# Wide cross attention with 77 keys a head laid out in 80 rows instead of 96, on one NeuronCore of Trainium2

## The reference

```python
def _L1_xattn_ref(x, context, ln_gamma, ln_beta, w_q, w_kv, w_out, b_out, gate):
    NUM_HEADS, DIM_HEAD = 16, 64
    xn = _layernorm(x, ln_gamma, ln_beta)
    q = (xn @ w_q).reshape(B, SQ, NUM_HEADS, DIM_HEAD)
    k, v = jnp.split(context @ w_kv, 2, axis=-1)
    ...
    scores = jnp.einsum('bqhd,bkhd->bhqk', q * DIM_HEAD ** (-0.5), k)
    attn = jax.nn.softmax(scores, axis=-1)
    out = jnp.einsum('bhqk,bkhd->bqhd', attn, v).reshape(B, SQ, INNER)
    out = out @ w_out + b_out
    return out * jnp.tanh(gate[0])
...
x = x + _L1_xattn_ref(_layernorm(x, axis=-1), ctx_1024, ...)
```

## Time and profile before

| what | value |
|---|---|
| median of 3 runs | 1561.71 us (1556.27 to 1563.02) |
| span of the profiled execution | 1523.6 us |
| median less that span | 38.1 us |
| busy: TensorE / ScalarE / VectorE / GpSimd | 93% / 55% / 60% / 43% |
| the stage's steps, from the first values to the last weighted sum | from 1008 to 1371 us of the span |
| share of the chain that ended last, L3137 / L3103 / L3128 | 6% / 6% / 3% |

### The profile page before, as it was taken

The page is one execution under the profiler, slowest core; times in us unless marked ns, Lnnn a source line. Parts: engine busy times, 40 slices in busy tenths (PEclk is TensorE's granted clock), DMA queues, the critical chain, the costliest instruction groups (busy, mean ns, idle before and its releaser), DMA issues.

```text
span 1523.6 us, 38875 instructions
## 1 busy us (share of the span) xinstructions
PE 1419.2 (93%) x14805; PEld 1097.5 (72%) x14805; DVE 920.5 (60%) x2386; ACT 837.5 (55%) x1622; POOL 660.8 (43%) x678
## 2 busy tenths in 40 slices
PE   6999999996999999999699998899999999998997
PEld 5776767675777876887466666678888888885864
DVE  3334444434789975434679998775666767656223
ACT  4545554443777875545267776555555556542531
POOL 3244444334234652006677876532234444433034
PEclk9999999998999999999789999999999999999999
DMA  5020320000357632237000000000000000001323
GB/s 160 17 64 8 100 92 28 8 5 1 142 203 274 229 130 72 78 118 274 19 12 2 2 2 2 14 2 6 7 6 8 11 11 7 9 11 41 103 69 87
DMA packets 97824, 92.65 MB, mean 61 GB/s; under 512 B 21869, under 2 KB 71658, under 8 KB 97386
## 3 DMA queue, kind: packets, MB, share of 16 engines
q1 hardware_dynamic: 93034, 80.71, 16.3%
q0 software_dynamic: 4608, 9.45, 2.0%
HBM read 31.92 MB, written 58.21 MB: 59 GB/s over the span
## 4 chain that ended last, share of the span: by engine, by line
PE 57%; issue 14%; POOL 13%; DVE 8%; ACT 4%; DMA 2%; SPq 1%; POOLq 0%; DVEq 0%; ACTq 0%
PE bank L3137 6%; PE bank L3103 6%; PE bank L3097 4%; PE bank L3116 4%; PE bank L1538 4%; POOL s_p L1217 4%; PE bank L1554 4%; PE bank L3128 3%; PE bank L854 2%; PE bank L2505 2%; PE bank L2515 2%; PE bank L874 2%; POOL s_level L467 2%; PE bank L827 2%; POOL s_rows L3564 2%
## 5 line engine op out<-in xcount | busy, mean ns | idle before, releaser
L2887 POOL TENSOR_TENSOR s_p<-s_p,s_inverse 128x616 f32<-128x616 f32 x64 | 78.3, 1229 | 221.5 <-DVE s_inverse L3024 221.5
L1324 ACT COPY s_pT<-bank 77x512 f32<-77x512 f32 (+1 forms) x256 | 135.1, 584 | 71.0 <-PE bank L1538 70.7
L1538 PE MATMUL bank<-ident,s_p 128*77 128x128 f32 (+1 forms) x1024 | 142.2, 287 | 17.0 <-ACT s_p L1315 10.3
L1538 PEld LDWEIGHTS bank<-ident,s_p 128*77 128x77 f32 (+1 forms) x1024 | 117.8, 149 | 45.7 <-ACT s_p L1315 28.9
L1217 POOL TENSOR_TENSOR s_p<-s_p,s_peak 128x1024 f32<-128x1024 f32 x64 | 120.2, 1898 | 33.9 <-DVE s_peak L1408 33.9
L1315 ACT ACTIVATE s_p<-s_p 128x616 f32<-128x616 f32 (+1 forms) x128 | 111.2, 889 | 32.2 <-POOL s_p L1217 27.7
L720 DVE TENSOR_TENSOR s_aT<-bank,s_weight 128x512 f32<-128x512 f32 x64 | 44.3, 692 | 98.8 <-PE bank L864 82.3
L3008 DVE TENSOR_REDUCE s_peak<-bank 128x8 f32<-128x616 f32 x64 | 50.7, 792 | 79.3 <-PE bank L3116 79.3
L2944 ACT ACTIVATE s_p<-s_p 128x616 f32<-128x616 f32 x64 | 46.5, 727 | 82.0 <-DVE s_p L3012 81.9
L1394 DVE TENSOR_TENSOR s_p<-bank,pos_bias 128x1024 f32<-128x1024 f32 x64 | 77.6, 1217 | 21.4 <-PE bank L1527 21.4
L3103 PE MATMUL bank<-pos_bias,s_ctx 128*32 128x128 f32 x3072 | 90.5, 274 | 0.0
(11 more groups left out here) (363 smaller groups left out, 3543.3 us busy)
## 6 DMA issues: line engine op xcount, KB each, us to landing
sorted_tokens<-s_zero SPq DMA_DIRECT2D x4, 5632.0 KB, 19.6
sorted_tokens<-s_zero SPq DMA_DIRECT2D x8, 2560.0 KB, 16.3
routed_tokens<-s_routed SPq DMA_DIRECT2D x24, 256.0 KB, 2.4
s_tokens<-sorted_tokens SPq DMA_DIRECT2D x48, 64.0 KB, 1.8
s_rows<-sorted_tokens SPq DMA_DIRECT2D x48, 64.0 KB, 1.8
x_all<-x SPq DMA_DIRECT2D x8, 256.0 KB, 3.1
w_s_gateup<-s_gateup SPq DMA_DIRECT2D x1, 2048.0 KB
out<-x_all SPq DMA_DIRECT2D x8, 256.0 KB, 2.6
```

What stands on the lines that cost most here:

```text
L1324: nc.scalar.copy(pT[0:keys, b % 2, 4 * q:4 * q + 4, :].rearrange("m h t -> m (h t)"), bank[0:keys, flip_bank("p", b, q), :]).then_inc(drai ...
L1538: last = nc.tensor.transpose(bank[0:keys, into, j * T:(j + 1) * T], p[:, b % 2, 4 * q + j, :], core.ident[:, :])
L2887: nc.gpsimd.tensor_tensor(part, part, inverse[:, b % 2, heads].unsqueeze(2).to_broadcast([P, HU, M]), ALU.mult).then_inc(share_ready, 1)
```

## The change

A head takes `MP` = 80 rows instead of 96, so the 16 heads take 10 tiles instead of 12, in three banks of 4, 4 and 2 tiles (`BANKS5`). 80 rows are two and a half pieces of 32: 8 of the 40 lane pieces of a batch lie across two heads. Such a piece is made by two products that accumulate into the same lane, each with zero columns where the other has keys; for that the context has 16 zero columns ahead of its 77 (`LEFT`) and 19 behind. `lane_pieces()` deals the products of each lane out in turns.

```diff
-MP = 96
+MP = 80
 QUAD = 4
 TILES5 = H * MP // P
-PER_QUAD = TILES5 // QUAD
+LEFT = 16
+WIDE = LEFT + 3 * LANE
+BANKS5 = [range(k, min(k + QUAD, TILES5)) for k in range(0, TILES5, QUAD)]
+LAST5 = len(BANKS5) - 1
...
 def lane_pieces():
-    per_head = MP // LANE
-    return [(k // 4, LANE * (k % 4), k // per_head, LANE * (k % per_head)) for k in range(QUAD * per_head)]
+    lanes = [[] for _ in range(LANES)]
+    for k in range(TILES5 * LANES):
+        head, row = divmod(LANE * k, MP)
+        if row + LANE <= MP:
+            lanes[k % LANES].append((k // LANES, head, LEFT + row, True, True))
+        else:
+            lanes[k % LANES].append((k // LANES, head, LEFT + row, True, False))
+            lanes[k % LANES].append((k // LANES, head + 1, LEFT + row - MP, False, True))
+    return [(LANE * lane, *piece) for turn in zip(*lanes, strict=True) for lane, piece in enumerate(turn)]
...
             for step in range(BATCH + 2):
-                for q in range(QUAD):
+                for q in range(len(BANKS5)):
                     if q % 2 == 0 and step < BATCH:
                         exp_of(step, q // 2)
                     if 1 <= step <= BATCH:
                         keep_values(step - 1, q)
                 for q in range(QUAD):
-                    if 1 <= step <= BATCH:
+                    if 1 <= step <= BATCH and q < len(BANKS5):
                         keep_pT(step - 1, q)
                     if heads_in(step):
                         keep_key(step // G + 1, heads_in(step)[q])
...
-            def values_of(b, q):
-                into, g = ring.fill(pe, "v", b, q), b // G
-                for tile, lane, head, row in lane_pieces():
-                    last = nc.tensor.matmul(bank[lane:lane + LANE, into, tile * D:(tile + 1) * D],
-                                            ctx[:, g % 3, b % G, row:row + LANE], vo[:, QUAD * q + head, :],
-                                            start=True, stop=True, tile_position=(0, lane))
-                last.then_inc(filled, 1)
+            def values_of(b):
+                g, into = b // G, {}
+                for k, (lane, tile, head, column, start, stop) in enumerate(pieces):
+                    q = tile // QUAD
+                    if q not in into:
+                        into[q] = ring.fill(pe, "v", b, q)
+                    last = nc.tensor.matmul(bank[lane:lane + LANE, into[q], tile % QUAD * D:(tile % QUAD + 1) * D],
+                                            ctx[:, g % 3, b % G, column:column + LANE], vo[:, head, :],
+                                            start=start, stop=stop, tile_position=(0, lane))
+                    if k == ends[q]:
+                        last.then_inc(filled, 1)
...
             def flip_p(b, q):
-                pe.wait_ge(share_ready, 2 * b + q // 2 + 1)
+                pe.wait_ge(share_ready, 2 * b + (1 if q == 0 else 2))
...
-                for j in range(PER_QUAD):
+                for j in BANKS5[q]:
...
             def weigh(b):
-                pe.wait_ge(drained, max(place["p", b, QUAD - 1], place["v", b, QUAD - 1]) + 1)
+                pe.wait_ge(drained, max(place["p", b, LAST5], place["v", b, LAST5]) + 1)
```

More of the change, by code:

```diff
@@ L2781, in stage5, with values @@
         folded_away = (w.s5_wvT, w.s5_wo, w.s1_wq, w.s1_wk)
-        def values(b, q):
-            return folded_away[b % 2 * 2 + q // 2][:, q % 2 * PER_QUAD:(q % 2 + 1) * PER_QUAD, :]
+        def values(b, tiles):
+            first = tiles[0] % H1
+            return folded_away[b % 2 * 2 + tiles[0] // H1][:, first:first + len(tiles), :]
         sem = core.plain_semaphore
@@ L2828, in stage5 @@
             for q in range(QUAD):
-                if step:
+                if step and q < len(BANKS5):
                     take("p", step - 1, q)
@@ L2853, in _ @@
                 if g >= 3:
[L2854 to L2855 removed]
+                    sp.wait_ge(filled, place["v", G * (g - 2) - 1, LAST5] + 1)
+                sp.dma_start(ctx[:, g % 3, :, LEFT:LEFT + M],
                              ctxT_dram[:, g * GM:(g + 1) * GM].rearrange("c (n m) -> c n m", m=M)
@@ L2930, in keep_values @@
                     act.wait_ge(weighed, b - 1)
-                nc.scalar.copy(values(b, q).rearrange("p j d -> p (j d)"),
-                               bank[:, ring_bank("v", b, q), 0:PER_QUAD * D]).then_inc(drained, 1)
+                nc.scalar.copy(values(b, BANKS5[q]).rearrange("p j d -> p (j d)"),
+                               bank[:, ring_bank("v", b, q), 0:len(BANKS5[q]) * D]).then_inc(drained, 1)
             def keep_pT(b, q):
@@ L2937, in keep_pT @@
                     act.wait_ge(weighed, b - 1)
-                nc.scalar.copy(pT[:, b % 2, PER_QUAD * q:PER_QUAD * (q + 1), :].rearrange("p j t -> p (j t)"),
-                               bank[:, ring_bank("p", b, q), 0:PER_QUAD * T]).then_inc(drained, 1)
+                tiles = BANKS5[q]
+                nc.scalar.copy(pT[:, b % 2, tiles[0]:tiles[0] + len(tiles), :].rearrange("p j t -> p (j t)"),
+                               bank[:, ring_bank("p", b, q), 0:len(tiles) * T]).then_inc(drained, 1)
             def exp_of(b, u):
@@ L3010, in soften @@
                 if b >= 2:
-                    dve.wait_ge(filled, place["p", b - 2, QUAD - 1] + 1)
+                    dve.wait_ge(filled, place["p", b - 2, LAST5] + 1)
                 nc.vector.tensor_tensor(p[:, b % 2, heads, 0:M].rearrange("p (g j) m -> p g j m", j=QUAD), scores,
@@ L3097, in key_of @@
                 nc.tensor.matmul(bank[:, into, 0:GM].rearrange("p (n m) -> p n m", m=M), kq[:, h, :],
-                                 ctx[:, g % 3, :, 0:M], start=True, stop=True).then_inc(filled, 1)
-            def values_of(b, q):
-                into, g = ring.fill(pe, "v", b, q), b // G
-                for tile, lane, head, row in lane_pieces():
-                    last = nc.tensor.matmul(bank[lane:lane + LANE, into, tile * D:(tile + 1) * D],
-                                            ctx[:, g % 3, b % G, row:row + LANE], vo[:, QUAD * q + head, :],
-                                            start=True, stop=True, tile_position=(0, lane))
-                last.then_inc(filled, 1)
+                                 ctx[:, g % 3, :, LEFT:LEFT + M], start=True, stop=True).then_inc(filled, 1)
+            pieces = lane_pieces()
+            ends = [max(k for k, piece in enumerate(pieces) if piece[1] in tiles) for tiles in BANKS5]
+            def values_of(b):
[9 more added lines that the diff above has]
+                        last.then_inc(filled, 1)
             def scores_of(b):
@@ L3123, in flip_p @@
             def flip_p(b, q):
-                pe.wait_ge(share_ready, 2 * b + q // 2 + 1)
+                pe.wait_ge(share_ready, 2 * b + (1 if q == 0 else 2))
                 into = ring.fill(pe, "p", b, q)
-                flat = p[:, b % 2, QUAD * q:QUAD * (q + 1), :].rearrange("p h m -> p (h m)")
-                for j in range(PER_QUAD):
-                    last = nc.tensor.transpose(bank[:, into, j * T:(j + 1) * T], flat[:, j * P:(j + 1) * P],
-                                               core.ident[:, :])
+                flat = p[:, b % 2, :, :].rearrange("p h m -> p (h m)")
+                for j in BANKS5[q]:
+                    last = nc.tensor.transpose(bank[:, into, j % QUAD * T:(j % QUAD + 1) * T],
+                                               flat[:, j * P:(j + 1) * P], core.ident[:, :])
                 last.then_inc(filled, 1)
             def weigh(b):
-                pe.wait_ge(drained, max(place["p", b, QUAD - 1], place["v", b, QUAD - 1]) + 1)
+                pe.wait_ge(drained, max(place["p", b, LAST5], place["v", b, LAST5]) + 1)
                 if b:
@@ L3137, in weigh @@
                     last = nc.tensor.matmul(bank[:, OUT, 0:D], pT[:, b % 2, j, :],
-                                            values(b, j // PER_QUAD)[:, j % PER_QUAD, :], start=(j == 0),
+                                            values(b, [j])[:, 0, :], start=(j == 0),
                                             stop=(j == TILES5 - 1))
@@ L3156, in _ @@
                 if 1 <= step <= BATCH:
-                    for q in range(QUAD):
-                        values_of(step - 1, q)
+                    values_of(step - 1)
                 for q in range(QUAD):
-                    if 1 <= step <= BATCH:
+                    if 1 <= step <= BATCH and q < len(BANKS5):
                         flip_p(step - 1, q)
```

5 lines of the change are left out of this document (3 added, 2 removed).

## The result

The changed kernel takes 1552.80 us (median of 13 runs, 1544.53 to 1556.74) against 1562.02 us of the kernel before (13 runs): a ratio of 0.9945, with a 95% interval of 0.9932 to 0.9959. The forecast of 1552.8 us was met, and the gain is just above the half per cent that I had named as what can be told from no change.

What follows compares the result with a forecast made beforehand. TensorE was taken as the bound, with ScalarE's ring of banks able to hold it up. Weighted sum -14.3, transposes and keys +5.9, step 1 -0.3, steps without keys -0.2: -8.9 us, so 1552.8 us, range 1546 to 1560.

Steps and rivals of the forecast that it cites:

- The weighted sum: 10 products for 12 on TensorE, four instructions fewer a batch, counting in full: -14.3 us in 32 batches.
- The values: Same 48 products and 96 instructions a batch on TensorE, 2.76 us as before: no change.
- the slower rival: Accumulating products of pieces across two heads wait for each other: 1566 to 1616 us; chance 5%.
- ScalarE's queue: Times after first values instruction: values copies start 1.37, 2.47 and 3.56, second exponential 2.94, last copy done 3.93 us.
- The rival with a larger fixed cost: ScalarE copies: all 0.265 us of the shortest fixed, each copy 0.1 us longer, 8.1 us lost: 1561 us; chance 3%.
- Transposes and keys: TensorE's turns in the 27 steps with keys: 0.11 us gained, 0.33 lost to stalls, 0.22 longer each: +5.9 us.
- p1's stall: Second transpose group waits for the last values copy, behind the second exponential on ScalarE: 0.19 us a step.
- The second stall: Third key waits for ScalarE's copy of the second transpose group: 0.14 us a step.
- Two transposes less are worth 0.11: In a step with keys, two transposes fewer on TensorE save 0.11 us, against 0.33 of stalls.
- Steps without keys: Steps 28 to 32: transposes end almost as before (-0.03 us a step), last weighted sum about 0.1 earlier; together -0.2 us.
- The 38.1 us around the span: Time outside the profiled 1523.6 us span, against the 1561.71 us median; taken to stay unchanged.
- No stalls: Rival: ScalarE early enough that TensorE never waits in the ring, 8.9 us come back: 1543.9 us; chance 13%.

Runs made afterwards that it cites:

- the run with both waits removed: The change with both exponentials ahead of the values copies on ScalarE and ring turns p0 k0 p1 k1 k2 p2 k3: 1539.93 us, ratio 0.9869 to the kernel before.

## Why the prediction was right, point by point

The mechanism was right: the removed products of the weighted sum count in full, and the ring takes part back at the two places named, p1 behind v2 and e1, and k2 behind the copy of p1. That the median came out at 1552.8 us to the hundredth is luck: two terms of the sum were off by 0.14 us a step or more each and cancelled, and the profiles show less of a gain than the times do.

- **The weighted sum** is worth what was said: 2.23 us in the chain, and 13.3 us alone (forecast 14.3).
- **The values** stay at 2.76 us. Products that accumulate into the same lane four products apart do not wait for each other; the slower rival is out.
- **ScalarE's queue** was right to 0.01 us at all five points. The copy of 256 columns, which no row of before showed, takes 0.363 us for the values (0.372 forecast by the straight line), as the groups of copies by shape show; that of transposes takes 0.382:

```profile
L2951 ACT COPY s_pT<-bank 128x512 f32<-128x512 f32 x64 | 37.4, 595 | 0.3 <-PE bank L3148 0.2
...
L2943 ACT COPY w_s_k<-bank 128x256 f32<-128x256 f32 x16 | 5.8, 363 | 0.0
```

 The rival with a larger fixed cost is out. The Trainium skill's page "ScalarE: Activation LUTs" (Rules for kernel authors) budgets about 0.3 us plus 0.83 ns an element for an ACTIVATE whose bias is a pointer operand; worked out for 256 columns that would be, as an estimate, 0.51 us. The instruction here is a COPY and takes 0.363.
- **Transposes and keys**: the forecast net of +0.22 us a step was measured as +0.24 (0.45 less in the weighted sum, 0.21 less in all), but two of its numbers were off and cancelled. A group of four transposes takes 0.44 us and not 0.49: the 0.123 came from a run of twelve. So without stalls the step would have been shorter, 10.42 and not 10.56. And p1's stall is 0.33 and not 0.19: k0 ends at 3.77, not 3.87, and p1's loads come 0.12 us after the copy's end, where I had taken 0.03 from a key. The second stall, 0.14, was 0.13 to 0.16. Together the stalls cost 0.49 and not 0.33.
- **"Two transposes less are worth 0.11"** was too little. From 11.12 to 10.42 us the step loses 0.70, of which 0.45 is the weighted sum; the 0.25 left are the two transposes and the 0.06 that e1 had cost before. The 0.11 came from pricing the transposes of after at 0.123 and taking those of before as measured, about 0.11 each; the forecast's "19 to 20 us" for all removed products price the two at about 0.2. The 0.14 that is missing here (3.8 us in 27 steps) stands against the 0.16 that is missing in the stalls. In the kernel before, where the ring was in balance, the run with one transpose in p3 shows them to be worth nothing.
- **Steps without keys** were sized wrong: steps 28 and 29 gain 0.26 us each instead of 0.48 (9.89 and 10.03 before, 9.63 and 9.77 after). Step 30, without routing at its end, gains 0.45 as forecast. In the other two the routing's products at the step's end use the ring as well, and wait for the copies of p behind e1, which I had followed only to the last transpose:

```profile
1368.80 0.97 PEld L3442 LDWEIGHTS bank<-w_s_routerT,w_s_w2T 128*128 128x128 f32 x8 [0.22 <-ACT s_pT L2951]
```

- **The 38.1 us around the span** were an artefact of holding one execution against a median of others. The sum stood on the steps and took no harm.
- **No stalls** (13%) did not come about by itself; the run with both waits removed shows what it would have been, 1539.9 us and not 1543.9; its steps without keys and its hole are shorter too. The Trainium skill's page "Perfetto Trace Analysis" (Optimization Strategy) says that consistent bubbles can mean too little SBUF or PSUM for the next tile. The trace agrees in so far as the gaps stand at the same two places in every step with keys, with a ring of three banks. But both went by another order, without a further bank, and no run here tries a further one.

The sum of -8.9 us stands against 9.2 us measured (6.4 to 10.6 by the interval), of which the stage's profiles show 6.6: the steps with keys gave 5.5 instead of 6.0, and the end of the stage 1.1 instead of 2.9, where the hole took 1.2 us more than in the second profile of before and steps 28 and 29 fell short by 0.4. No row shows the rest of 2.6 us. To the end of the program the profiles show only 3.9 to 5.4 us, less than the interval's lower end; what is missing lies ahead of the fifth stage or between executions, and its cause stays open.

## What to carry to other kernels

Where an engine fills a small ring of banks and another empties it, time taken off the filling engine counts in full outside the turns of the ring. Inside, it can be lost to a wait, as in p3 of before; see how long a bank is away (fill, hand over, copy, hand back) and put at least that much other work between two uses. Wider copies empty more at a time, but the first comes later, so what stands between them in the emptying engine's queue can move onto the path: here an exponential that cost 0.06 us a step before cost 0.33 after. Two reorderings without a product less, e1 first and k2 ahead of p2, took 0.49 us off a step, where the removed tiles had taken 0.21.

## What the runs showed of the hardware

GpSimd's scatters can go with a hold-up of TensorE where no data passes between them: in step 32 values that take 2.83 us stretch to 5.4 us (1390.68 to 1396.08) with three scatters at 1390.77, 1392.10 and 1393.37, TensorE going on in packets of 3 to 6 matmuls some 0.7 us apart, and with the scatters held back they take 2.83 again. In the two runs with the exponentials first, with scatters 0.46 us ahead of these values and 1.46 us into them, they take 3.38 us; in the first profile of before, with scatters at -0.06 and 1.46 us, 2.83. What decides it is not shown.
